# Moving the first batch's last Q groups and the second batch's input split ahead of a stage seam, in a fused cross-attention kernel

## The reference, cut to what matters

```
q = x @ wq.T + bq ; k = ctx @ wk.T + bk ; v = ctx @ wv.T + bv      (split into 16 heads)
p = softmax(q k^T / sqrt(32) + mask * PAD)
out = layernorm(p v + x) * gamma + beta
```

## Time and profile before

| | us |
|---|---|
| median of 3 runs | 1146.4 |
| lowest, highest | 1145.2, 1146.83 |
| profiled execution, its own time | 1145.06 |
| its span, first to last instruction | 1143.3 |
| TensorE, VectorE, POOL, ScalarE busy | 1095.9, 941.6, 770.0, 726.6 |

### The profile page before, as it was taken

The page is one execution under the profiler, slowest core; times in us unless marked ns, Lnnn a source line. Parts: engine busy times, 40 slices in busy tenths (PEclk is TensorE's granted clock), DMA queues, the critical chain, the costliest instruction groups (busy, mean ns, idle before and its releaser), DMA issues.

```text
span 1143.3 us, 26963 instructions
## 1 busy us (share of the span) xinstructions
PE 1095.9 (96%) x7541; PEld 989.2 (87%) x7541; DVE 941.6 (82%) x1782; ACT 726.6 (64%) x1136; POOL 770.0 (67%) x668
## 2 busy tenths in 40 slices
PE   7999889999999999999999999999999999999984
PEld 7888679889988988888899889898888989898973
DVE  6988478888888888888888888888888888888886
ACT  3221366777677777767667777776776767777651
POOL 4999513667666766777676667666667776776565
PEclk9999999999999999999999999999999999999996
DMA  6744554455555556555555655565556555555433
GB/s 220 259 151 172 185 148 104 112 159 152 147 147 158 143 156 159 159 137 145 142 138 143 159 158 143 140 160 148 149 159 159 149 136 147 137 137 123 122 99 135
DMA packets 176906, 171.34 MB, mean 150 GB/s; under 512 B 110004, under 2 KB 111556, under 8 KB 176868
## 3 DMA queue, kind: packets, MB, share of 16 engines
q1 hardware_dynamic: 167044, 145.36, 44.5%
q10 hardware_dynamic: 9824, 25.50, 10.1%
HBM read 96.76 MB, written 48.85 MB: 127 GB/s over the span
## 4 chain that ended last, share of the span: by engine, by line
PE 56%; DVE 14%; issue 8%; ACT 7%; ACTq 3%; DVEq 0%
PE q_ps L811 21%; PE o_ps L856 16%; PE t_ps L842 9%; PE s_ps L828 7%; DVE row_max L981 4%; ACT pt L1153 3%; DVE probs L990 2%; PE s_ps L831 2%; DVE stats L915 2%; DVE q_b L971 2%; ACT q_a L1136 2%; ACTq L1148 2%; ACTq L1146 2%; DVE q_c L968 1%; ACT q_b L1138 1%
## 5 line engine op out<-in xcount | busy, mean ns | idle before, releaser
L856 PE MATMUL o_ps<-v_tiles,pt 128*128 128x66 f32 x2520 | 314.0, 272 | 1.0 <-DVE attn L907 0.8
L856 PEld LDWEIGHTS o_ps<-v_tiles,pt 128*128 128x128 f32 x2520 | 302.8, 192 | 6.7 <-issue 4.0
L981 DVE TENSOR_REDUCE row_max<-s_ps 128x8 f32<-128x616 f32 x256 | 204.1, 797 | 119.0 <-PE s_ps L831 110.0
L1116 ACT ACTIVATE probs<-probs 128x616 f32<-128x616 f32 x256 | 183.6, 717 | 135.6 <-issue 68.9
L1090 POOL TENSOR_TENSOR x_lo<-xT_raw,x_hi 128x512 fp32r<-128x512 f32 x124 | 158.2, 1277 | 163.8 <-ACT x_hi L1126 163.2
L1058 POOL TENSOR_TENSOR attn<-attn,x_rows 128x512 f32<-128x512 f32 x124 | 158.8, 1281 | 153.5 <-DVE attn L907 153.5
L1153 ACT COPY pt<-t_ps 128x512 f32<-128x512 f32 (+1 forms) x320 | 186.9, 584 | 82.1 <-PE t_ps L842 76.6
L811 PE MATMUL q_ps<-x_lo,wq_hi 128*128 128x512 f32 x504 | 220.6, 438 | 4.6 <-PEq L148 4.3
L842 PE MATMUL t_ps<-ident,probs 128*128 128x128 f32 (+1 forms) x1280 | 200.4, 280 | 12.4 <-ACT pt L1153 5.0
L990 DVE TENSOR_TENSOR probs<-s_ps,row_max 128x616 f32<-128x616 f32 x256 | 204.7, 800 | 5.7
L811 PE MATMUL q_ps<-x_hi,wq_lo 128*128 128x512 f32 x504 | 199.8, 396 | 0.0
(11 more groups left out here) (96 smaller groups left out, 1676.7 us busy)
## 6 DMA issues: line engine op xcount, KB each, us to landing
xT_raw<-in_xT SPq DMA_DIRECT2D x128, 256.0 KB, 3.6
x_rows<-in_x SPq DMA_DIRECT2D x32, 1024.0 KB, 6.3
out<-y SPq DMA_DIRECT2D x128, 256.0 KB, 2.7
k_scratch<-k_out SPq DMA_DIRECT2D x8, 1232.0 KB, 5.1
k_ac<-k_scratch SPq DMA_DIRECT2D x256, 38.5 KB, 5.6
q_a<-q_a ACTq DMA_DIRECT2D x64, 128.0 KB, 3.4
q_c<-q_a ACTq DMA_DIRECT2D x64, 128.0 KB, 3.6
q_b<-q_b ACTq DMA_DIRECT2D x64, 128.0 KB, 3.6
```

The costliest lines, as they stand in the source:

```text
L856: mm = pe.matmul(bank_of(b, t)[:, col:col + tile_cols[i]], pt[h][0:w, i, P * t:P * t + P], v_tiles[v_buffer(b, h)][0:w, i, 0:tile_cols[i]] ...
L981: dve.tensor_reduce(row_max[:, u, :].rearrange("p (j h) -> p j h", j=2), score_heads(t), AX.X, ALU.max).then_inc(max_ready, 1)
L1116: act.activation(probs[h][:, t, :], probs[h][:, t, :], ACT.Exp).then_inc(exp_done, 1)
```

## The change

The first batch's Q is made in stage one altogether, four groups. `q_ps0` and `q_ps1`, stage two's Q banks, are allocated ahead of both stages and serve as `k_ps0` and `k_ps1` in stage one; groups go to banks 2, 3, 0, 1. The first three groups are read out and get their low parts in stage one; the fourth is read out at the head of ScalarE's step 0 in stage two, with the moves of its half behind it, and its low parts are written by VectorE at s = 1 as before. The moves of the first half are issued before the third group's readout.

The second batch's x is split in stage one. `x_hi1` and `x_lo1` are allocated ahead of both stages, and `wk_hi` and `wk_lo` are now the same memory. ScalarE casts the four pieces when all K products are done; POOL writes `x_lo1` piece by piece between the value masks of chunk 3. In stage two the splits of batch 1 fall away, and SP's wait for them is met at the start. VectorE's wait for gamma and beta goes from its start to the two functions that use them.

```diff
+        x_hi1 = sb(whole, "x_hi1", [P, KC, T], F32R)
+        x_lo1 = sb(whole, "x_lo1", [P, KC, T], F32R)
+        q_ps = [ps(whole, f"q_ps{i}", [P, BANK]) for i in range(2)]
...
-            wk_hi = sb(one, "wk_hi", [P, KC, D], F32R)
-            wk_lo = sb(one, "wk_lo", [P, KC, D], F32R)
+            wk_hi, wk_lo = x_hi1, x_lo1
...
-            k_ps = [ps(one, f"k_ps{i}", [P, BANK]) for i in range(NG)]
+            k_ps = q_ps + [ps(one, f"k_ps{i}", [P, BANK]) for i in range(2, NG)]
+            def first_q(g):
+                return k_ps[(g + 2) % NG]
...
# POOL, stage one, in keep_values, after the mask of tile j
+                        if c == CHUNKS - 1 and j < KC:
+                            pool.wait_ge(x_hi_ready, KC + j + 1)
+                            pool.tensor_tensor(x_lo1[:, j, :], xT_raw[:, j, :], x_hi1[:, j, :], ALU.subtract
+                                               ).then_inc(x_lo_ready, 1)
...
# ScalarE, stage one
+                act.wait_ge(k_done, 2 * NG * CHUNKS)
+                for k in range(KC):
+                    act.wait_ge(xT_loaded[k], 2 * DMA)
+                    act.copy(x_hi1[:, k, :], xT_raw[:, k, :]).then_inc(x_hi_ready, 1)
-                for g in range(2):
+                for g in range(NG - 1):
+                    if g == 2:
+                        move_first_half()
                     act.wait_ge(q_done, g + 1)
...
# VectorE, stage one
-                for g in range(2):
+                for g in range(NG - 1):
                     dve.wait_ge(q_hi_ready, 2 * g + 2)
...
# TensorE, stage one
-                for g in range(2):
+                for g in range(NG):
...
-            def in_phase_one(b, g=0):
-                return isinstance(b, int) and b == 0 and g < 2
+            def in_phase_one(b):
+                return isinstance(b, int) and b == 0
+            def drained_in_phase_one(b, g):
+                return isinstance(b, int) and b == 0 and g < NG - 1
+            def split_in_phase_one(b):
+                return isinstance(b, int) and b <= 1
...
# VectorE, stage two: in scale_row and in finish_output, and no longer ahead of the steps
+                    dve.wait_ge(scale_loaded, 2 * DMA)
-                dve.wait_ge(scale_loaded, 2 * DMA)
...
# ScalarE, stage two
+                        if s == 0 and isinstance(a, int) and a == 0:
+                            high_q(0, NG - 1)
+                            move_q(0, 1)
```

More of the change, by code:

```diff
@@ L327, in _ @@
                 pool.wait_ge(wq_lo_ready, 1)
-                pool.wait_ge(x_lo_ready, KC)
+                pool.wait_ge(x_lo_ready, 2 * KC)
             @block.scalar
@@ L350, in keys, with move_first_half @@
                                  ).then_inc(k_hi_copied, 1)
+                def move_first_half():
+                    act.wait_ge(q_hi_ready, 4)
+                    act.dma_start(q_a[QW:P, 0:2, :].bitcast(F32), q_a[0:DH, 0:2, :].bitcast(F32)).then_inc(q_moved[0], DMA)
+                    act.dma_start(q_c[QW:P, 0:2, :].bitcast(F32), q_a[DH:2 * DH, 0:2, :].bitcast(F32)).then_inc(q_moved[0], DMA)
+                    act.dma_start(q_b[0:DH, 0:2, :].bitcast(F32), q_b[QW:P, 0:2, :].bitcast(F32)).then_inc(q_moved[0], DMA)
                 def load_mask():
@@ L528, in _ @@
                 dve.wait_ge(consts_loaded, DMA)
-                for g in range(2):
+                for g in range(NG - 1):
                     dve.wait_ge(q_hi_ready, 2 * g + 2)
-                    dve.scalar_tensor_tensor(out=q_c[0:QW, g, :], in0=k_ps[g][0:QW, :], scalar=bq_col[0:QW, g:g + 1],
+                    dve.scalar_tensor_tensor(out=q_c[0:QW, g, :], in0=first_q(g)[0:QW, :], scalar=bq_col[0:QW, g:g + 1],
                                              in1=q_a[0:QW, g, :], op0=ALU.add, op1=ALU.subtract
                                              ).then_inc(q_lo_ready, 1)
-                    dve.scalar_tensor_tensor(out=q_b[DH:2 * DH, g, :], in0=k_ps[g][QW:P, :],
+                    dve.scalar_tensor_tensor(out=q_b[DH:2 * DH, g, :], in0=first_q(g)[QW:P, :],
                                              scalar=bq_col[QW:P, g:g + 1], in1=q_b[QW:P, g, :],
@@ L637, in xattn @@
         with ExitStack() as two:
-            x_hi = [x_hi0, sb(two, "x_hi1", [P, KC, T], F32R)]
-            x_lo = [x_lo0, sb(two, "x_lo1", [P, KC, T], F32R)]
+            x_hi = [x_hi0, x_hi1]
+            x_lo = [x_lo0, x_lo1]
             k_ac = [k_ac0, sb(two, "k_ac1", [P, 2, NG, 3, SW], F32R)]
@@ L662, in xattn @@
             t_ps = ps(two, "t_ps", [P, BANK])
-            q_ps = [ps(two, f"q_ps{i}", [P, BANK]) for i in range(2)]
             o_ps = ps(two, "o_ps", [P, BANK])
@@ L865, in step @@
                         ahead, g, part = q_of_step(s)
-                        if real(a + ahead) and not in_phase_one(a + ahead, g):
+                        if real(a + ahead) and not in_phase_one(a + ahead):
                             q_half(a + ahead, g, part, (par + ahead) % 2)
@@ L1043, in step @@
                         ahead, g, part = q_of_step(s)
-                        if part == 1 and real(a + ahead) and not in_phase_one(a + ahead, g):
+                        if part == 1 and real(a + ahead) and not drained_in_phase_one(a + ahead, g):
                             q_low(a + ahead, g)
@@ L1100, in step @@
                         for k in range(KC):
-                            if X_STEPS[k] == s and real(a + 2):
+                            if X_STEPS[k] == s and real(a + 2) and not split_in_phase_one(a + 2):
                                 split_x(a + 2, k, par)
@@ L1171, in step @@
                         for k in range(KC):
-                            if X_STEPS[k] == s and real(a + 2):
+                            if X_STEPS[k] == s and real(a + 2) and not split_in_phase_one(a + 2):
                                 high_x(a + 2, k, par)
                         ahead, g, part = q_of_step(s)
-                        high = part == 1 and real(a + ahead) and not in_phase_one(a + ahead, g)
+                        high = part == 1 and real(a + ahead) and not in_phase_one(a + ahead)
                         if high:
```

10 lines of the change are left out of this document (3 added, 7 removed).

## The result

| | before | after |
|---|---|---|
| median, us | 1145.98 | 1141.01 |
| runs | 16 | 16 |
| ratio of the runs | 1 | 0.9955 (0.994 to 0.997) |
| profiled execution, its own time | 1145.06 | 1141.87 |
| its span | 1143.3 | 1139.7 |

By the ratio the changed kernel is 5.2 us faster, with an interval of 3.4 to 6.9; the forecast was 5.4. Two of the 16 runs of the kernel before took 2143.64 and 2719.68 us, far outside the other fourteen (1143.71 to 1151.65, median 1145.5). The profiled execution of the changed kernel took 0.9 us more than its median and that of the kernel before 0.9 us less, so the two profiles lie only 3.2 us apart.

A forecast was written before the change was run, and what follows sets the result against it. TensorE, busy 1095.9 of 1143.3 us, was taken to set the pace from the second batch on. -5.8 + 0.4 = -5.4 us from 1145.06 gave 1139.7 profiled, 1141.0 for the median; range 1139.4 to 1144.5.

The forecast's parts named there:

- The seam: Between stages one and two: stage two starts at 133.8 instead of 130.8, 3.0 us lost, VectorE's low parts last.
- the cover: Stage one: x casts fit ScalarE's idle; delayed masks and stores tie with VectorE's 133.1; no cost, up to 0.3 us.
- The first maximum: VectorE's first work in stage two: at 135.0 instead of 138.76; moving the gamma and beta wait avoids 2.9 us.
- The failed step: Batch 0's second-half Q moves: issued until 137.05, landing by 142.0 at the same 4.99 us, 2.6 to spare.
- the moves become the wait: Rival, 10%: second-half moves, beside gamma, beta, x and keys, land at 147.0; 2.5 us lost, 1143.5.
- the -5.8 of that step: ScalarE's readout of batch 1's second Q group: at 147.85 instead of 153.61, 5.8 us earlier.
- The clock: Before TensorE's first turn: some 2.1 us idle may halve its granted clock, pricing 0.4 us off the gain.
- the clock costs nothing at the seam itself: Start of stage two: a slightly later clock fall costs nothing, as VectorE and ScalarE bind; low from first scores, 0.7.
- The chain itself: Stage two's start, from first maximum through batch 1's readouts on VectorE and ScalarE until TensorE rules again: -5.8 us.
- the gain was not given back: Rival, 9%: loads rather than TensorE pace the batches, so an earlier start changes nothing: 1145.5 to 1147.
- the stores did not end the stage: Rival, 4%: delayed value stores end stage one; each us landed after 133.1 is lost, 1149.0 if at 141.1.
- the clock did not stay low until batch 1: Rival, 5%: TensorE's clock stays low through the first batch until about 145; gain about 3.6 us, 1142.8.

The follow-up runs named there:

- number 12: Changed kernel with POOL's four x_lo pieces behind all five value masks instead of between them: 1140.41 us, ratio 0.9947 to the kernel before.
- Number 3: Changed kernel with VectorE's wait for gamma and beta put back at the start of stage two: 1144.33 us, ratio 0.9988 to the kernel before.
- number 4: Changed kernel with the third batch's x loaded at the end of stage one, behind the last value store: 1141.16 us, ratio 0.9951.
- number 5: Changed kernel with gamma and beta loaded behind the first values and POOL's wait for them moved to step 2: 1139.6 us, ratio 0.9936.
- number 11: Kernel of number 5 with the last two of four x pieces also issued behind POOL's clearing of the value tiles: 1140.1 us, ratio 0.9943.
- numbers 8: Changed kernel with the fourth Q group read out, its low parts made and the second half's moves issued in stage one too: 1144.77 us, ratio 0.9981.
- 10: Kernel of number 5 run again unchanged, side by side with the changed kernel: 1140.13 us, ratio 0.9941 to the kernel before.
- numbers 6: Changed kernel with the third batch's four x pieces loaded one by one between the last value stores: 1144.27 us, ratio 0.9979.
- 7: Changed kernel with x pieces loaded between the last value stores, and gamma and beta behind the first values: 1144.52 us, ratio 0.9979.

## Why the prediction was right, and where not

The total was right: 5.4 forecast, 5.2 measured. Step by step, measured from the last K cast to take out the 0.9 us by which this execution was late before the change's first instruction:

- **The seam.** Forecast 3.0 us later, with VectorE's low parts last: 2.7 later (15.8 against 13.1), VectorE last, stage two 0.3 behind it instead of 0.7. The x casts, the masks (last one 127.89 to 128.94) and the stores lay where the cover was named; number 12 shows the stores' slack. SP waited 1.9 us for them behind the last issue, a little under the low end of my bounds (2.0).
- **The first maximum.** Forecast at 135.0, 17.3 behind the K cast; measured 17.0. Number 3 shows what the moved wait is worth: with it kept, 3.8 of 5.2 us go.
- **The failed step: "they land by 142.0 if they take the same 4.99; needed is 144.6, so they have 2.6 to spare".** The 4.99 runs from the end of the last issue; by the same measure they took 7.9 (8.5 against 5.4 from its start) and landed at 145.5. I had carried over a duration from a place where 1 MB of x had been issued 2 us ahead of the moves, with the keys among them; at the new place gamma and beta stood ahead as well, and all 1.5 MB was issued within 3 us. Numbers 4, 5 and 11 show that what is ahead of the moves sets this: with less of it they landed 4.8, 6.3 and 2.6 us after issue. The rival "the moves become the wait" held 10% and named the mechanism with its bound (147.0). So batch 1's second readout came at 150.71 instead of 147.85, and the -5.8 of that step was -2.9 in the profile, -3.8 by the distance from the K cast.
- **The clock.** I priced a 2 us gap before the first turn at 0.4. That gap was not there; the one before the scores was 3.75, with 6.3 us at half clock behind it, and it made the readout wait 1.03 us for TensorE. In number 11, where a gap of 2.46 us did stand before the turn, the clock was at half from about 145.4 to 148.3, and the second readout waited only 0.16 us for TensorE. That the clock costs nothing at the seam itself held where it fell there: from the first maximum to the readout of batch 1's first group it is 7.4 and 7.6 us in numbers 8 and 4, and 7.6 in number 5 at full clock.
- **The chain itself** was right wherever the transfers are out of the way. In number 5 the first maximum, the readout of batch 1's first group, the next maximum and the second readout stand at 134.93, 142.50, 145.49 and 148.09; forecast were 135.0, 142.6, 145.5 and 147.85.

That the total came within 0.2 us although this step failed is in part luck. Measured from the K cast, the first product comes 3.5 and 4.5 us earlier than before in the two profiles of the changed kernel, and the first maximum of the last batch 4.2 and 5.0; by the timed runs the gain is 5.2 and 7.6. The chain without the price of the clock, -5.8, is what numbers 5, 10 and 11 did (5.8, 5.9 and 5.8 earlier at the first product), and their timed gains are 7.3, 6.8 and 6.5. So in all five the timed runs gave 0.7 to 3.1 us more than the profiles. There is only one profile of the kernel before, and the ends scatter by 4.3 us; why the two measures differ stays open.

The Trainium skill (DMA: Bandwidth & Descriptors, "Queues, rings and completion order") says that a DMA engine takes turns between the queues that have work, packet by packet, and I read that as protection from a backlog on the other queue. Nothing here speaks against the turns: the last piece of x, issued just ahead of the last move, took 9.5 us and the move 8.5. But the protection did not come. The last move of a half took 2.3 us from issue to landing at a DMA share of 0.31 (the first half, before), 2.9 behind the last value stores (changed), 6.3 beside 1 MB of x, and 8.5 beside 1.5 MB.

The other rivals: the gain was not given back (the batch period is 30.76 before and 30.74 after), the stores did not end the stage, and the clock did not stay low until batch 1.

## What to carry to other kernels

When work that waited on several things is freed of one of them, price the parts together: here each half of the change alone brought 1.0006 and 0.9993, both 0.9955. When a load moves earlier, list every transfer that is in flight at its new place and ask who waits for each; operands that are used late (gamma and beta) should not be waited for at a stage's start (number 3), nor stand first in the queue (numbers 5 and 10: 1.4 to 2.4 us earlier to the first product than the changed kernel, though the timed runs did not settle it). Issuing a small transfer on the critical path ahead of the large ones suggests itself, but no run here tried it. A duration from the trace holds for the company that the instruction had there.

## What the runs showed of the hardware that I had not expected

- The last of three 128 KB moves landed between 2.3 and 8.6 us after issue, by what else was in flight, though that was on another engine's queue.
- The issue of a transfer can hold its engine: 2.21 and 2.56 us for one move on ScalarE in numbers 6 and 7 instead of 0.62, with the DMA share at 1.01 to 1.03 for 4 us before. At the same share in number 4 it did not.
- TensorE's clock fell to half (1.2 of 2.4 GHz) inside a gap of 0.99 us that came 0.9 us after one of 1.49 in number 5, and did not fall behind the single one of 1.35 us at the changed kernel's seam. The stretches, with the columns as above, of number 5:

```profile
144.40:147.40 3.00, 2.72 (x9) 2.33 (x10) 2.62 (x4) 1.57 (x4) 1.28 (x1) 0.50 0.21 34
```

and of the changed kernel:

```profile
134.60:138.00 3.40, 3.34 (x23) 3.07 (x24) 2.37 (x4) 1.50 (x3) 3.38 (x6) 1.00 0.73 146
```
